# Causal mask of the transposed scores as a GpSimd selection on the exponentials, with operand rows at a pitch of eight

## The reference, cut to what matters

```python
def _L0_attn_ref(x, W_qkv, q_scale, k_scale, W_out):      # B, S, D = 4, 512, 128; H = 16; Hd = 8
    q, k, v = jnp.split(jnp.einsum('bsd,de->bse', x, W_qkv), 3, axis=-1)
    q, k = _layernorm(q, q_scale), _layernorm(k, k_scale)  # then all three to (B, S, H, Hd)
    scores = jnp.einsum('bshd,bthd->bhst', q / jnp.sqrt(Hd), k)
    scores = jnp.where(future[None, None], jnp.finfo(scores.dtype).min, scores)
    ctx = jnp.einsum('bhst,bthd->bshd', jax.nn.softmax(scores, axis=-1), v)
    return jnp.einsum('bsd,de->bse', ctx.reshape(B, S, D), W_out)
```

## Time and profile before

| | |
|---|---|
| runs | 514.33, 515.88, 516.07 us; median 515.88 |
| profiled execution | 516.09 us; span from first to last instruction 514.4 us, 12569 instructions |
| granted TensorE clock, mean | 0.97 |
| busy PE / DVE / ACT / POOL | 467.6 / 390.3 / 355.9 / 188.4 us |
| chain that ended last | PE 61%, DVE 16%, ACT 8%, issue 4%, SP queue 3%, POOL 3%, DMA 2%, ACT queue 2% |

### The profile page before, as it was taken

One profiled execution on the slowest core, in us unless ns is written; L12 is line 12 of the kernel. 1 busy time (PEld: TensorE's weight loads), 2 busy tenths in 40 slices (PEclk: granted clock), 3 DMA queues, 4 the chain that ended last, 5 costly groups with the idle time before them and its releaser, 6 DMA issues.

```text
span 514.4 us, 12569 instructions
## 1 busy us (share of the span) xinstructions
PE 467.6 (91%) x4432; PEld 312.1 (61%) x4432; DVE 390.3 (76%) x1125; ACT 355.9 (69%) x909; POOL 188.4 (37%) x362
## 2 busy tenths in 40 slices
PE   5446999998999998999999999998999999999994
PEld 2324556754445655657687556666764666797784
DVE  3638988699799899975799899865887678547354
ACT  2212857776666878789677688995686779877953
POOL 7850000261102183253132242533223547734633
PEclk9567999999999999999999999999999999999998
DMA  6163210013210021120000100020000000000001
GB/s 163 46 218 99 79 45 4 26 51 86 68 29 8 15 64 33 40 59 11 13 2 15 52 24 3 7 60 19 4 13 12 1 2 3 0 2 1 11 2 31
DMA packets 27202, 18.21 MB, mean 35 GB/s; under 512 B 8333, under 2 KB 26885, under 8 KB 27013
## 3 DMA queue, kind: packets, MB, share of 16 engines
q1 hardware_dynamic: 22101, 13.14, 9.5%
q10 hardware_dynamic: 5040, 4.27, 2.7%
HBM read 5.58 MB, written 1.05 MB: 13 GB/s over the span
## 4 chain that ended last, share of the span: by engine, by line
PE 61%; DVE 16%; ACT 8%; issue 4%; SPq 3%; POOL 3%; DMA 2%; ACTq 2%; POOLq 0%; DVEq 0%
PE psum L1030 9%; PE psum L1372 5%; PE psum L1349 5%; PE psum L1083 5%; PE psum L1142 4%; PE psum L1110 4%; ACT EX L1526 3%; PE psum L1389 3%; PE psum L1132 3%; PE psum L1285 3%; PE psum L1129 3%; DVE nmax L1778 3%; DVE nmax L1783 2%; DVE Y_rest L1939 2%; PE psum L1400 2%
## 5 line engine op out<-in xcount | busy, mean ns | idle before, releaser
L1526 ACT ACTIVATE EX<-psum 128x1024 f32<-128x1024 f32 (+1 forms) x128 | 117.8, 976 | 8.4 <-PE psum L1116 4.9
L1783 DVE TENSOR_REDUCE nmax<-psum 128x2 f32<-128x768 f32 (+1 forms) x96 | 77.5, 861 | 12.3 <-PE psum L1089 12.0
L1778 DVE TENSOR_REDUCE nmax<-psum 128x4 f32<-128x616 f32 (+1 forms) x80 | 67.6, 876 | 9.9 <-PE psum L1083 9.6
L1083 PE MATMUL psum<-K,Q 48*128 48x154 bf16 (+4 forms) x512 | 52.7, 275 | 11.4 <-DMA K<-parts 6.8
L993 POOL TENSOR_TENSOR GP<-REST,xrs 128x512 f32<-128x512 f32 (+1 forms) x48 | 32.7, 704 | 41.1 <-DVE xrs L2012 24.2
L1110 PE MATMUL psum<-Q,K 51*128 51x512 bf16 (+3 forms) x320 | 44.0, 316 | 4.0 <-DMA Q<-mrows 1.5
L1427 ACT COPY pvraw<-psum 128x512 f32<-128x512 f32 x32 | 18.6, 583 | 34.9 <-PE psum L1142 24.9
L1609 ACT ACTIVATE REST<-psum,nxmax 128x154 f32<-128x154 f32 x96 | 36.2, 393 | 9.1 <-DVE nxmax L2007 8.3
L928 POOL TENSOR_SCALAR rstd_rest<-moments_rest 128x2 f32<-128x2 f32 x32 | 8.0, 249 | 88.6 <-DVE moments_rest L1826 88.1
L1083 PEld LDWEIGHTS psum<-K,Q 48*128 48x128 bf16 x512 | 21.0, 95 | 30.7 <-issue 20.5
L1142 PE MATMUL psum<-EX,V 128*32 128x256 f32 (+3 forms) x512 | 37.8, 435 | 0.0
(11 more groups left out here) (333 smaller groups left out, 1184.5 us busy)
## 6 DMA issues: line engine op xcount, KB each, us to landing
Q<-xparts SPq DMA_DIRECT2D x48, 64.0 KB
Q<-parts SPq DMA_DIRECT2D x42, 64.0 KB
K<-parts SPq DMA_DIRECT2D x42, 64.0 KB
X<-in_x SPq DMA_DIRECT2D x4, 256.0 KB, 3.0
Q<-in_L_xattn_Wkv ACTq DMA_DIRECT2D x1, 1024.0 KB, 5.8
Q<-mrows SPq DMA_DIRECT2D x64, 6.0 KB
K<-xkparts SPq DMA_DIRECT2D x48, 19.2 KB
out<-XB_rest SPq DMA_DIRECT2D x6, 128.0 KB, 1.8
```

The source lines that it names most:

```text
L1083: last = mm(to[:, r, at:at + n], Q6[a][p, b % 2, 2 * g + jj, P * q:P * q + P], K6[a][p, b % 2, 2 * g + jj, 0:n], start=True, stop=bool(a))
L1526: drains(nc.scalar.activation(dst, src, ACT.Exp), key)
L1778: last = vec.tensor_reduce(nmax[:, :, :, q], src[:, :, 0:2 * n].rearrange("p r (j k) -> p r j k", j=2), AX.X, ALU.max, negate=True)
L1783: last = vec.tensor_reduce(nmax[:, :, jj, q], src[:, :, at:at + P * (q + 1)], AX.X, ALU.max, negate=True)
```

## The change

The diff does five things. First, the four mask matmuls of each ST piece (line 1116) go, with `maskT` and its making; instead POOL applies `affine_select` to the diagonal block of both heads in `EX` after the exponential (new `diagonal`, one instruction of 128 x 2 x 128 elements for each of the eight pieces), and `values` waits for `ex_masked` instead of for the exponential. The mask matmuls of S stay. Second, slot s of feature f moves from row 64 r + 6 f + s to row 8 x group + s of all 128 partitions, so one DMA places a slot for both halves, from 128 partitions to 16; the maxima go to rows 6, 30, 54, 78, 102, 126, by one DMA. The matmuls span 64 rows instead of 48 or 51, so unused rows must be zero or one: `Q6` is filled with zeros and `K6` with ones over all partitions, and from batch 2 on one DMA clears the maximum rows for each operand use. Third, the placement is shared by `shares` between y = 0 (SP) and y = 1 (at the start ACT), three slots each. Fourth, the fills move: those of `K6[1]` go ahead of the first norm, `late_zeros` waits for `qk_normed` (DVE's normalisation of q in batch 0), `Q6[1]` is filled after the setup products, and the load of x for batch 1 is issued third. Fifth, `MERGE` and `BANK_OF` are new throughout.

```diff
-SPLIT_ROWS = SLOTS * HD
-MAX_ROW = SPLIT_ROWS
-ST_ROWS = MAX_ROW + 3
+ROW_STEP = 8
+MAX_ROWS = slice(SLOTS, P, 3 * ROW_STEP)
+def shares(w, y):
+    parts_ = (Q_PARTS, K_PARTS)[w]
+    return [(s, parts_[s]) for s in sorted(range(SLOTS), key=lambda s: parts_[s])[y::2]]
...
 MERGE = (
-    "rrrrrwwrrrlrrlluurrrrrlsssssssssssrrrluuttttstlluussspptststtpuussltvssppttssuutttps"
+    "rrrrrrrrrrlluwwrrrrrrllsssssuuuvssssssrrttutttsuussspptlsttsttllluuspsspptsswttsttup"
...
+        def placement(b, a, w, s, part):
             n = C if a and w else S
-            to = (Q6, K6)[w][a][TILE * r + s:TILE * r + SPLIT_ROWS:SLOTS, b % 2, :, 0:n]
-            parts_ = (xkparts if w else xparts)[:, part, 0:n] if a else parts[:, w, part, :]
-            return to, parts_[TILE * r:TILE * r + TILE, :]
+            to = (Q6, K6)[w][a][s:P:ROW_STEP, b % 2, :, 0:n]
+            return to, (xkparts if w else xparts)[:, part, 0:n] if a else parts[:, w, part, :]
...
             load_x(0)
             sp.dma_start(wqkv, L0_attn_W_qkv).then_inc(qkv_loaded, 16)
+            load_x(1)
...
+            def place_self(b, y, w):
...
+                elif y == w == 0:
                     filled(sp, (b - 2, "ST", 0, NQ - 1, T_UNITS[0] - 1))
+                    sp.dma_start(*clearing(b, 0)).then_inc(qk_placed, 16)
+                for s, part in shares(w, y):
                     sp.wait_ge(part_ready[0][part], 2 * b + 1 + w)
+                    sp.dma_start(*placement(b, 0, w, s, part)).then_inc(qk_placed, 16)
...
                 drained(sp, (b, "mT", a, g))
-                for r in R:
-                    p = TILE * r + MAX_ROW
-                    sp.dma_start(Q6[a][p:p + 3, b % 2, 2 * g:2 * g + 2, :].rearrange(
-                        "p j t -> p (j t)"), mrows[24 * r:24 * r + 24, parity(b, a, g), :]
-                        ).then_inc(max_placed[a], 16)
+                sp.dma_start(Q6[a][MAX_ROWS, b % 2, 2 * g:2 * g + 2, :].rearrange(
+                    "p j t -> p (j t)"), mrows[:, parity(b, a, g), :]).then_inc(max_placed[a], 16)
...
             pool.wait_ge(wqkv_ready, 1)
-            for r in R:
-                nc.gpsimd.memset(words(K6[0][TILE * r + 32:TILE * r + TILE, 0, :, :]),
-                                 TWO_ONES).then_inc(zeros_ready, 1)
+            for w, value in enumerate((0.0, TWO_ONES)):
+                nc.gpsimd.memset(words((Q6, K6)[w][0][:, 0, :, :]), value).then_inc(zeros_ready, 1)
...
             pool.wait_ge(first_zeros_ready, 1)
+            step(nc.gpsimd.memset(words(K6[1].rearrange("p b h t -> p (b h) t")), 0.0))
+            step(nc.gpsimd.memset(K6[1].rearrange("p b h t -> p (b h) t").bitcast(F32)[
+                :, :, 0:C // 2], TWO_ONES))
             def late_zeros():
+                pool.wait_ge(qk_normed, 1)
+                for w, value in enumerate((0.0, TWO_ONES)):
+                    step(nc.gpsimd.memset(words((Q6, K6)[w][0][:, 1, :, :]), value))
...
+            def diagonal(b, a, g, u):
+                if a:
+                    return
+                drained(pool, (b, "ST", 0, g, u))
+                first = ex_slot(b, 0, g, u)
+                for at, jj, k in SELF_T_PIECES[u]:
+                    block_ = EX[:, first:first + 2, at:at + P]
+                    last = nc.gpsimd.affine_select(out=block_, in_=block_, compare_op=ALU.is_ge,
+                                                   fill=0.0, base=0, pattern=[[0, 2], [1, P]],
+                                                   channel_multiplier=-1)
+                last.then_inc(ex_masked, 1)
...
                 for at, jj, k in ([(0, u, 0)] if a else SELF_T_PIECES[u]):
                     n = S - P * k
                     for r in R:
-                        p = slice(TILE * r, TILE * r + ST_ROWS)
+                        p = slice(TILE * r, TILE * r + TILE)
                         last = mm(to[:, r, at:at + n], K6[a][p, b % 2, 2 * g + jj, P * k:P * k + P],
-                                  Q6[a][p, b % 2, 2 * g + jj, P * k:S], start=True, stop=bool(a))
-                    for e in (() if a else R):
-                        for r in R:
-                            p = slice(TILE * r, TILE * r + TILE)
-                            last = mm(to[:, r, at:at + TILE * (e + 1)], ident2[p, e, :],
-                                      maskT[p, e, 0:TILE * (e + 1)], start=False, stop=e == 1)
+                                  Q6[a][p, b % 2, 2 * g + jj, P * k:S], start=True, stop=True)
...
             def values(b, a, g):
-                drained(pe, (b, "ST", a, g, T_UNITS[a] - 1))
+                if a:
+                    drained(pe, (b, "ST", a, g, T_UNITS[a] - 1))
+                else:
+                    pe.wait_ge(ex_masked, T_UNITS[0] * (NQ * b + g + 1))
```

More of the change, by code:

```diff
@@ L355 @@
+    "123576401235764012357640123576401235764"
 )
@@ L477, in build @@
         maskS = sb("maskS", [P, 2, P], BF16)
-        maskT = sb("maskT", [P, 2, P], BF16)
         X0 = sb("X0", [P, 2, NB, D])
@@ L751, in place_self @@
                     filled(sp, (b - 2, "ST", 0, NQ - 1, T_UNITS[0] - 1))
-                for part in range(3):
+                    sp.dma_start(*clearing(b, 0)).then_inc(qk_placed, 16)
+                for s, part in shares(w, y):
                     sp.wait_ge(part_ready[0][part], 2 * b + 1 + w)
-                    for s, slot_part in enumerate((Q_PARTS, K_PARTS)[w]):
-                        if slot_part == part:
-                            sp.dma_start(*placement(b, 0, r, w, s, part)).then_inc(qk_placed[r], 16)
@@ L759, in place_cross @@
-            def place_cross(b, r, w):
+                    sp.dma_start(*placement(b, 0, w, s, part)).then_inc(qk_placed, 16)
+            def place_cross(b, y, w):
                 if b == 0:
                     sp.wait_ge(late_zeros_ready, 1)
-                    filled(sp, (0, "wM", SETUP_PRODUCTS - 1))
-                elif b >= 2:
+                    sp.wait_ge(cross_rows_ready, 1)
+                elif b >= 2 and y == 0 and w:
                     filled(sp, (b - 2, "ST", 1, NQ - 1, T_UNITS[1] - 1))
-                for part in range(3):
+                    sp.dma_start(*clearing(b, 1)).then_inc(cross_placed, 16)
+                for s, part in shares(w, y):
@@ L769, in place_cross @@
                     sp.wait_ge(part_ready[1][part], 2 * b + 2 - w)
-                    for s, slot_part in enumerate((Q_PARTS, K_PARTS)[w]):
-                        if slot_part == part:
-                            sp.dma_start(*placement(b, 1, r, w, s, part)).then_inc(cross_placed[r], 16)
+                    sp.dma_start(*placement(b, 1, w, s, part)).then_inc(cross_placed, 16)
             def mT(b, a, g):
                 if b or g:
-                    sp.wait_ge(max_placed[a], 32 * (NQ * b + g))
+                    sp.wait_ge(max_placed[a], 16 * (NQ * b + g))
@@ L1430, in flat, with place_first @@
                 return t.rearrange("p a b -> p (a b)")
-            def place_first(b, r, w):
-                if b or not r:
+            def place_first(b, y, w):
+                if b or not y:
                     return
-                act.wait_ge(zeros_ready, 2)
-                for part in range(3):
+                act.wait_ge(zeros_ready, 1 + w)
+                for s, part in shares(w, y):
                     act.wait_ge(part_ready[0][part], 1 + w)
-                    for s, slot_part in enumerate((Q_PARTS, K_PARTS)[w]):
-                        if slot_part == part:
-                            act.dma_start(*placement(0, 0, r, w, s, part)).then_inc(qk_placed[r], 16)
+                    act.dma_start(*placement(0, 0, w, s, part)).then_inc(qk_placed, 16)
                 if w:
```

111 lines of the change are left out of this document (49 added, 62 removed).

## The result

The changed kernel takes 511.59 us (median of 5 runs, 510.60 to 512.36) against 515.88 before, a ratio of 0.9927 with a 95% interval of 0.9901 to 0.9952: 3.8 us faster by the ratio, where 9.4 were forecast. The time lies inside the range, but the gain is small, and the experiments show that its sources were other ones than the sum named.

What follows compares the result with a forecast made beforehand. PE was taken as the bound in most self-turn stretches, DVE in others, single steps before 36 us. Terms 9.3 - 3 - 1.5 + 4.4 + 1 - 0.5 = 9.7 us off 516.1; forecast 506.5 us, range 494 to 519.

Steps and rivals of the forecast that it cites:

- Mask matmuls removed, 9.3 us: PE in the self turns: 128 pieces at 0.09 us are 11.5 us, of which 9.3 count as gain; bounds 7 and 11.5.
- PE leads: Stretches 160 to 210 and 266 to 316 us: PE busy 48.2 and 49.6 of 50 us, DVE close behind.
- two stretches taken off in the sum: 36 to 56 and 100 to 133 us, where DVE leads: 24 pieces, so 2.2 us of removed masks buy little.
- Selections added, 3 us: Product with V waits for the last unit's two selections: 0.3 us a turn, 3 us lost, between 0 and 10.
- DVE blocked, 1.5 us: Selections on POOL delay small DVE instructions in the chain of maxima: 1.5 us lost on the path, bounds 0 and 6.5.
- the ring: Rival: ten turns pay 1.0 us each as the ten exponential slots are full, DVE loses 6.5; 515.5 us, chance 0.13.
- POOL's queue: Rival: selections stand behind POOL's layer-norm waits and hold the product with V, 16 us; 523 us, slower, chance 0.17.
- Blocking by the fill: Clearing DMAs and the fill of `Q6[1]` take POOL time ahead of the next selection: 0.5 us lost, 0 to 2.
- Start, 4.4 us: Before the first scores: unblocked DVE normalisation gains 2.9 us, fewer K placement issues on ACT 1.5; bounds 2 and 5.
- One DMA for the maxima, 1 us: On the way to ST one of two 0.73 us issues goes: 1 us gained, from 0.5 us at most a wait.
- placement inside it: Later batches' placement issues on SP fall from 24 to 12, freeing the queue for the maxima; inside that 1 us.
- Order tables, 0 with bounds of 5: Effect of the new order can't be read from any row: taken as 0, bounds -5 to +5 us.

Runs made afterwards that it cites:

- start line: Kernel before with one line more, POOL's second fills at the start wait until DVE has normalised q: 513.54 us, ratio 0.9944.
- selections aside: Changed kernel, 128 selections from a constant into an unread spare tile, product with V not waiting for them, ST unmasked: 506.13 us; without POOL's wait for the exponential 508.08.

## Why the prediction was right or wrong

The steps in a line, from the ratios and with the medians: start line -2.9 us (513.5), placement and rest of the start -2.6 (510.5), tables -5.1 (505.5), mask from PE to POOL +6.9 (511.6). The order of the steps matters: the tables before the placement would be +24.5.

- *Mask matmuls removed, 9.3 us.* Wrong, and the step that failed most: 0 in the old order and 2.8 in the new one. The price of 0.09 us a piece was read rightly (PE's busy time fell by 6.5 us, the union with neighbours included), but "PE leads" was taken from busy shares of 96% to 99%. The self turns run round a loop (exponentials, product with V, exponentials), which the part on the selections described and whose period of 9.1 us in batch 0 it had read; the part on the masks did not ask whether PE or this loop ends last there. Without the masks the products with V of batch 0 still came about every 9.1 us (68.28, 77.42, 86.41), and from the second product to the sixteenth, 14 of the 16 turns, only 1.2 us were gained (247.2 against 248.4). The clock took something too: in this execution it was 0.50 instead of 0.66 from 30 to 50 us, and the first product started 2.3 us later (58.26). A smaller slip: the two stretches taken off in the sum hold 31 of the 128 pieces and not 24, which makes 8.7 us of the 9.3.
- *Selections added, 3 us, and DVE blocked, 1.5 us.* The duration was right (0.42), the sum was 4.5 and the runs show 8.9. The wait that the 3 us priced is hardly there: in batch 0, where the ring was feared, the way from the first to the fourth product is 1.1 us longer than with PE masks, and masking the last unit on PE gained nothing. What was mis-sized is the term of blocking, taken as many small delays of half a selection each. Without the normalisation on the queue the changed kernel is 6.8 us shorter. The blocks that lie on the path are two long ones, 2.5 and 2.3 us, because selections that had queued behind the normalisation ran in a row, and DVE stood until the row was over; a low clock of PE followed each. The list of POOL's steps could have shown the queueing. The rival "POOL's queue" named it, but with the waits for layer norms as its cause, PE's wait as its way and 16 us as its price; the cause was the normalisation's 8.4 us of own work, met twice, and the way led over DVE.
- *Blocking by the fill.* Missed. The sum gave the fill 0.5 us and looked only for selections behind it, not for DVE's copies beside it; it is worth 2.5 us with the mask on PE. The rows for that were on the table: the same lock had been read at the start. The Trainium skill, page "SBUF — State Buffer", section "Who interferes with whom", lists copies, casts and tensor_scalar as those that can block against GpSimd and tensor_reduce as one that on this chip never does; the trace agrees, with 2.65 us for a copy of 0.21, 2.90 for a cast of 0.43, and 860 and 876 ns for the maxima as before.
- *Start, 4.4 us.* The mechanism was right and the start line's share too (2.9 us in time; maxima 2.8 us earlier). The whole start came out larger, 7.0 us, as half the issues stand before the first scores and PE's eight projections of batch 1 took 3.72 instead of 5.45 us: the granted clock was 0.76 from 20.9 to 24.7 us, where they ran, and 0.51 from 23.8 to 29.2 us before. ACT's three K issues end behind the last copy, as said.
- *One DMA for the maxima, 1 us, and placement inside it.* Mis-sized: some 3 us in the old order (which holds the rest of the start as well), 32 us in the new.
- *Order tables, 0 with bounds of 5.* Mis-sized: -5.1 us on the new placement, just past the bound, +24.5 on the old, and with selections the old tables cost 19.5 us. A table fits one kernel.

That the total of 511.6 was inside the range is luck, as two errors had different signs. The move of the mask was forecast as a gain of 4.8 us (9.3 less 4.5) and lost 6.9; start, placement, fill and tables were forecast at 4.9 us and gave 10.6.

## What to carry to other kernels

A busy share of 98% doesn't make an engine the bound: before a removed instruction is counted as gained time, look whether the period of the loop around it is held by a chain through other engines, and take the work out of the kernel as a test. When work is moved to a less busy engine, read that engine's queue for long blocks that it will stand behind, and then what the packed row behind such a block does to a neighbour whose instructions it holds; 50 us fitted into POOL's idle time by volume and still cost 8.9 us, where the matmuls that they replaced cost 2.8. A run that is to keep one of two costs has to be read in the trace: the selections aside were as many and stood at the same places, but the small gaps between them let DVE through. Time each part of a bundled change by itself and together with those it leans on: here one part lost 6 to 7 us behind the gains of three others, and the tables were worth -5 or +24.5 us, depending on the DMAs.

## What was not expected of the hardware

The granted clock was lower in the kernels with less work for PE. From 56 to 100 and from 100 to 133 us it was 1.00 before and 0.95 and 0.93 with the masks taken out, and the mean over the whole was 0.958 in the twelve executions without masks against 0.968 in the 23 of the kernel before beside them. In the changed kernel it was 0.90 from 95 to 128 us, where PE was busy for 26.9 of 33 us, and 0.78 from 115 to 127 us, where it was busy for 9.1 of 12. A mean below 1.00 is a mix of the levels of 2.4 and 1.2 GHz, so 0.010 less over 516 us are some 10 us more at the lower level, or at most 5 us of PE's work at the full one: an upper estimate of what the clock took back of the 9.3 us. The busy share alone does not tell it: with selections aside the clock was 1.00 from 116 to 125 us, where PE was busy for 7.4 of 9 us. That mask matmuls are partly paid by a clock that they keep is therefore likely and not shown.

The second is the size of a block. A DVE cast of 0.43 us stood for 2.5 us beside eight selections of about 0.4 us that followed each other without a gap, and for 0.15 us beside the eight that had small gaps between them (4.31 us in all). It waited for the row and not for one instruction.
